# Graph network in one kernel: in round 2 the target one-hots are multiplied by the edge weights on ACT, not on DVE

## What is computed

```
def _L1_gnn_ref(h, edge_norm, edge_types, src, dst, weight, bias):
    ht = jnp.einsum('ni,rio->nro', h, weight)
    msg = ht[src, edge_types] * edge_norm[:, None]
    out = jax.ops.segment_sum(msg, dst, num_segments=h.shape[0])
    return jax.nn.relu(out + bias)
...
x = _layernorm(x + _L0_gnn_ref(x, edge_index, edge_attr_16, ...))
x = _layernorm(x + _L1_gnn_ref(x, edge_weight, edge_type_8, src, dst, ...))
x = _layernorm(x + _L2_gnn_ref(x, edge_index, ...))
x = _layernorm(x + _L3_gnn_ref(x, edge_index, ...))
```

## Time and profile before

| | |
|---|---|
| median of 3 runs | 4695.95 us (4695.62 to 4703.1) |
| profiled execution, device time | 4692.29 us |
| its span in the trace | 4690.0 us |
| round 2, first to last window sums | 1139.67 to 2173.8 us |
| busy over the span | PE 3381.4, DVE 2355.6, ACT 1326.1, POOL 2446.8 us |
| chain that ended last, by engine | POOL 48%, PE 31%, issue 16%, DMA 2%, DVE 1%, ACT 1% |

### The profile page before, as it was taken

The page is one execution under the profiler, slowest core; times in us unless marked ns, Lnnn a source line. Parts: engine busy times, 40 slices in busy tenths (PEclk is TensorE's granted clock), DMA queues, the critical chain, the costliest instruction groups (busy, mean ns, idle before and its releaser), DMA issues.

```text
span 4690.0 us, 66657 instructions
## 1 busy us (share of the span) xinstructions
PE 3381.4 (72%) x22549; PEld 2229.8 (48%) x22549; DVE 2355.6 (50%) x5590; ACT 1326.1 (28%) x3135; POOL 2446.8 (52%) x2488
## 2 busy tenths in 40 slices
PE   3888888886677666674333333337888999999998
PEld 3554555453445444453232322326884555555554
DVE  6755555554555656554555555557882121121122
ACT  1233233332122222222444444447871000000000
POOL 3777777775777777775777777772330000000000
PEclk8999999998888888886555555557999999999999
DMA  3333444443333333333677777778877777777776
GB/s 107 105 118 120 127 135 131 124 126 110 91 98 94 103 102 100 96 96 102 197 201 196 197 200 195 199 196 290 308 260 282 278 277 288 288 274 278 286 291 227
DMA packets 506575, 855.11 MB, mean 182 GB/s; under 512 B 111387, under 2 KB 284487, under 8 KB 506228
## 3 DMA queue, kind: packets, MB, share of 16 engines
q1 hardware_dynamic: 338752, 542.03, 32.8%
q0 software_dynamic: 87808, 179.98, 15.2%
q10 hardware_dynamic: 79668, 128.70, 7.5%
HBM read 632.93 MB, written 217.55 MB: 181 GB/s over the span
## 4 chain that ended last, share of the span: by engine, by line
POOL 48%; PE 31%; issue 16%; DMA 2%; DVE 1%; ACT 1%; SPq 0%; ACTq 0%; POOLq 0%; DVEq 0%
POOL big L818 32%; POOL big L845 16%; PE psS L1884 11%; PE psA L1884 11%; PE psS L1539 4%; PE psA L1764 1%; PE ps L1830 1%; PE ps L1821 1%; ACT big L1224 1%; PE ps L1468 1%; PE psA L1574 1%; DMA big<-in_src_dram 0%; DMA big<-A_rows 0%; PE ps L1587 0%; PE ps L1611 0%
## 5 line engine op out<-in xcount | busy, mean ns | idle before, releaser
L818 POOL DMA_INDIRECT big<-xw_rows,srci x784 | 768.8, 981 | 308.5 <-issue 238.8
L818 POOL DMA_INDIRECT big<-ht_rows,reli x784 | 787.7, 1005 | 254.3 <-issue 238.7
L845 POOL DMA_INDIRECT big<-axt_rows,srci x784 | 749.7, 956 | 250.9 <-issue 238.7
L1539 PE MATMUL psS<-big 128*128 128x128 f32 x3136 | 502.6, 327 | 310.5 <-DMA big<-ht_rows,reli 305.6
L1539 PEld LDWEIGHTS psS<-big 128*128 128x128 f32 x3136 | 471.9, 238 | 380.4 <-DMA big<-ht_rows,reli 342.5
L901 POOL TENSOR_TENSOR xsb<-xsb,l3b2r 128x896 f32<-128x896 f32 x6 | 12.5, 2082 | 1114.3 <-DMA xsb<-x_keep 1114.3
L1884 PE MATMUL psS<-big,xsb 128*128 128x448 f16 x1372 | 485.1, 354 | 17.2 <-DMA big<-A_rows 17.2
L1884 PE MATMUL psA<-big,xsb 128*128 128x448 f16 x1372 | 485.1, 354 | 0.0
L1696 PE MATMUL ps<-identh,xsb 128*128 128x128 bf16 x784 | 101.4, 310 | 530.8 <-DVE xsb L2380 530.8
L1884 PE MATMUL psS<-big,acc 128*128 128x448 f16 x1372 | 483.6, 352 | 0.0
L1884 PE MATMUL psA<-big,acc 128*128 128x448 f16 x1372 | 483.6, 352 | 0.0
(11 more groups left out here) (299 smaller groups left out, 5086.3 us busy)
## 6 DMA issues: line engine op xcount, KB each, us to landing
big<-A_rows SPq DMA_DIRECT2D x112, 2744.0 KB, 13.6
A_rows<-xsb ACTq DMA_DIRECT2D x196, 416.0 KB
xg_rows<-big SPq DMA_DIRECT2D x98, 512.0 KB, 3.8
big<-xg_rows SPq DMA_DIRECT2D x98, 512.0 KB, 4.2
marks_rows<-big SPq DMA_DIRECT2D x98, 354.0 KB
big<-marks_rows SPq DMA_DIRECT2D x98, 354.0 KB, 5.5
big<-srcq_list SPq DMA_DIRECT2D x98, 256.0 KB
ht_rows<-big ACTq DMA_DIRECT2D x25, 512.0 KB, 2.9
```

Source lines behind the costliest of these rows:

```text
L818: pool.indirect_dma_start(ring[g % len(ring)][:, j * D:(j + 1) * D], None, table[:, :], bass.IndirectOffsetOnAxis(ap=lists[:, g * TPG + j: ...
L845: pool.indirect_dma_start(wide[g % NS][:, j, :], None, axt_rows[:, :], bass.IndirectOffsetOnAxis(ap=srci[:, g * TPG + j:g * TPG + j + 1], ...
L1539: m = pe.matmul(psS[b][:, 0:P], rows[b][:, j * P:(j + 1) * P], marks[b][:, j * P:(j + 1) * P], start=(j == 0), stop=(j == TPG - 1))
```

## The change

In round 2's branch `more < 1`, DVE only compares, and signals `r_ohraw`. ACT waits for that and multiplies the 8 tiles of the group's one-hots by their column of `wedge`, by eight activations in place (Copy with a scale), and signals `r_oh`. On ACT this stands before the loop for group 0, and for g + 1 behind `block_stage(g)` and `early_n2(g)`.

```
+            def weigh_onehots(g):
+                b = g % 2
+                act.wait_ge(r_ohraw[b], g // 2 + 1)
+                for j in range(TPG):
+                    ones_ = onehot[:, b, j * P:(j + 1) * P]
+                    m = act.activation(ones_, ones_, ACT.Copy, scale=wedge[:, g * TPG + j:g * TPG + j + 1])
+                m.then_inc(r_oh[b], 1)
             with act.If(more < 1):
+                weigh_onehots(0)
                 for g in range(NG):
                     if g + 1 < NG:
                         block_stage(g % 2, g // 2 + R2N)
                     early_n2(g)
+                    if g + 1 < NG:
+                        weigh_onehots(g + 1)
                 summed(R1)
...
                     bases[g] = load_base(it, b)
-                    make_onehots(b, bases[g], 0, it, it + R.w0, weights)
+                    if weights is None:
+                        make_onehots(b, bases[g], 0, it, it + R.w0, None)
+                    else:
+                        compare(b, bases[g], 0, it).then_inc(r_ohraw[b], 1)
```

## The result

Before 4696.39 us (median of 5 runs, 4695.62 to 4703.1), after **4811.56 us** (5 runs, 4809.4 to 4817.79): a ratio of 1.0243, 95% interval 1.0229 to 1.0257. The kernel became slower by 115 us. The forecast was 4775 in a range of 4735 to 4820, so the sign and the range held; of the 115 us it had 79. The profiled execution has a span of 4807.1 us, against 4690.0.

The account below looks back on a forecast made before the run. Gathers bound round 2 at 10.49 us per group; a 10.84 us ring takes over: 96 x 10.84, + 54 - 10, less 1007.35, is 77 us, 79 with the end; 4695.95 + 79 = 4775 us, range 4735 to 4820.

Parts of the forecast that it names:

- the ring: Window sums, block counts, casts, store issue, activations, next window sums: 10.84 us per ordinary group against the gathers' 10.49.
- Hand-over 3.07 us: From the last cast through store issue and eight activations on ACT to PE's next window sums: 3.07 us.
- Chunk work 54 us: ACT's other work per chunk of nodes, standing before the activations, lengthens the round by 54 us.
- So it is the nearest row, and I take it: Last cast taken to end 7.77 us after window sums began, from one group with 3.47 us of PE standstill.
- The relief of 10 us: After PE turns a chunk's sums, casts end at 6.15 us and not 7.77, six times: 10 us back.
- The end of the round: Last window sums come 2.75 us after the last comparison ended, where it was 1.36: 1.4 us more.
- POOL's wait: POOL waits for window sums from some 60% of the round on, some 30 us in total, costing nothing more.
- The product's removal worth nothing to the gathers: Taking the product off DVE gives POOL's gathers 0, since the comparison holds them and the product does not.
- The ring under the gathers: Rival, 6%: with full clock in nearly every group the gathers still set the pace and only the end counts: 4697 us.
- The gain by gathers held less: Rival, 2%: the gathers also lose stretching by DVE, up to 42 us: 4655 us.
- The slower clock: Rival, 5%: PE stays at the lower clock level through a whole group, 12.11 us per group: 4897 us.
- The branch for several windows: Rival, 1%: the program runs the branch where DVE keeps its product, so the change does nothing: 4696 us.

Follow-up runs that it names:

- e1: The changed kernel with ACT's eight activations of group g + 1 moved ahead of the casts of group g: 4688.82 us, ratio 0.9991.
- e10: The changed kernel plus 16 unread matmuls on PE behind the chunk step of every group of round 2: 4694.13 us, ratio 1.0003.
- e2: The changed kernel with the activations between the casts and ACT's chunk step: 4741.22 us, ratio 1.0098.
- e4: The changed kernel plus six unread matmuls on PE behind the block counts of 35 groups without a chunk step: 4794.13 us, ratio 1.0209.
- e5: The changed kernel plus twelve unread matmuls on PE in each of 35 groups without a chunk step: 4762.49 us, ratio 1.015.
- e8: The kernel before without DVE's product by the weights in round 2, nothing in its place (sums unweighted): 4692.16 us, ratio 1.0.
- e6: The kernel before with DVE's product by the weights put behind the block's one-hots: 4727.11 us, ratio 1.0074.
- e9: The changed kernel with a second set of eight activations per group in round 2, multiplying by 1.0: 5000.05 us, ratio 1.0658.
- e7: The kernel before with comparison and product of round 2 fused into eight one-tensor-input DVE instructions: 4728.18 us, ratio 1.0086.

## Why the prediction was right, and where its size was off

**The gathers bound the round, the ring takes over: right.** Runs e1 (ring away, nothing lost) and e10 show it; the window sums' idle time went from gathers to ACT and back.

**Hand-over 3.07 us: right**, 3.04 measured, in ordinary groups of after and e2, and of e4 and e5 where no gather came later. The activations cost 2.45 us, the row of the next stage. **Chunk work 54 us:** 50.

**"So it is the nearest row, and I take it" is the step whose size failed.** The 7.77 us to the last cast came from one group with a standstill of 3.47 us and was put down for 90 groups; measured were 8.10 in the mean of 96. Over 96 groups, with the next point, that is 96 x (8.10 - 7.67) = 41 us, more than the 36 that were missing. The row itself was not an odd one: the 21 groups of before with 3.3 to 3.9 us of standstill end their casts at 7.84 us in the mean. What failed is the premise that the standstill's length fixes the price. Over 7.77 us, the 32 us of casts in after lie like this: 10 us in the 56 groups with about the forecast's standstill (3.5 to 3.7 us, casts from 7.5 to 9.1, mean 7.95, nine of them at 9); 16 us in 20 groups with 4.4 us and more, nearly all behind chunk steps, which the forecast counted by their length alone ("3.6 us, every time"); and 7 us in 18 groups with less, twelve of which stood still for 3.2 to 3.4 us and have a mean of 8.49. Why groups with the same standstill differ stays open. That the clock is what lengthens them is shown by e10.

**The relief of 10 us did not come.** After PE has turned the chunk's sums, casts ended at 7.44 to 7.49 us and not at 6.15. The row at 2147.02 was one of several here too: in before, the groups right behind the six turnings of the long chunks end theirs at 6.03, 7.67, 6.04, 8.76, 6.04 and 7.68 us. The standstill right before the window sums is short, as forecast, but there is another ahead of the turning, and the window sums run at the lower level for most of their length:

```profile
1486.46 0.96 PE L1461 MATMUL psA<-ident,stT 128*128 128x128 f32 x7 [2.12 <-ACT stT L1004]
1488.77 3.37 PE L1549 MATMUL psS<-big 128*128 128x128 f32 x16 [1.35 <-issue]
```

**The end of the round:** 2.8 us and not 1.4. The window sums begin 2.65 us after the last comparison (before: 1.36), as forecast; the comparison itself stands 1.5 us later behind group 96.

**POOL's wait:** 77 us and not 30, because the lag was 36 us larger, and because the gathers were shorter, 988 ns (58 held by a comparison, for 33 us, where 81 were, for 39 us), so POOL was ahead sooner. It first waited in group 46 of 98, not in the last third. This cost nothing on the path, as forecast.

**The product's removal worth nothing to the gathers: right** (e8: 1.0, 0.999 to 1.0011), and for the reason given, its place. The forecast's words "the product does not" hold it up were too strong: it does where it stands alone (e6).

**The rivals.** The ring under the gathers, 6%, is what e10 shows with 0.97 of the clock. It needs full clock in nearly every group, as it said, and with the ring's own standstill no group of after has it. The gain by gathers held less did not show: e8 has the removal alone, at a ratio of 1.0. The slower clock, 5%, was part of what happened: one ordinary group in four of the first 15 took its 12.1 us, and it is the source of most of what was missing. The branch for several windows did not run: the activations are there.

## What to carry to other kernels

Before work is moved to an idle engine, look for the place on its queue, not for its idle time: behind an instruction that waits for the very consumer, it closes a ring, and ahead of it the same work is free (4811.56 against 4688.82 us). A standstill of TensorE costs twice, by itself and by the slower clock of what follows. Its length alone does not give the price (casts at 7.5 to 9.1 us after the same 3.6), so state it as a range, and take in the longer standstills that the other work in the ring makes. And what an instruction costs a gather depends on when the gather begins: two in a row may cost what one costs, and the same one moved apart 33 us more.

## What the runs showed of the hardware

- **TensorE's clock.** With 3.6 us of standstill in ordinary groups, the window sums took 2.6 to 3.76 us, most of them near the 3.75 of the lower level (1.2 GHz), and the granted clock was 0.80 in the stage table (after); behind useless matmuls, which left mostly 1.0 to 2.3 us, 79 of 96 groups had them at the upper (2.4 GHz, 2.02 us or little more), and it was 0.97 (e10). These matmuls gave the whole of the loss back.
- **The same standstill is followed by different clocks.** After 3.6 us each, casts ended at 7.76, 7.74, 7.62 and 9.08 us by turns (after); after 5.3 us each, they climbed from 8.18 to 8.87 over the first groups and from 7.6 to 8.8 behind each chunk (e9).
- **A standstill of 2.3 to 2.8 us** between fillers and window sums left the upper level on in some groups and not in others (e4: 11 of 35 with window sums of 2.02 us).
- **An activation with a column as scale** takes 389 ns for 128x128, one with a number 295 (in series 0.306 and 0.212 us each).
- **A gather with its list in SBUF** that begins some 0.05 us or more after the start of a running DVE instruction waits for that instruction and ends 0.82 us after it: by the comparison (before, 81 of 81 with more than 0.14 us of it left), by the product (e6, 96 of 96), and by instructions with one tensor input (e7, 37 of 39 begun 0.03 to 0.2 us in). One that begins earlier is not held (before, 0 of 8 in the comparison). Some wait for a whole series of instructions that follow each other without a gap, up to 3.34 us for a gather that otherwise takes 0.95 (e7).
